# Loading x a body ahead and placing its vector steps elsewhere in a conditioned mixture-of-experts layer

## The reference

```python
q = relu(cond @ W3 + b3)                       # one row of 512 per sequence
h = relu(((64 * x + x.sum(axis=1)) * q) @ W2 + b2)
scores = softmax(h @ gate_w.T)                 # 64 experts
w, i = top_k(scores, 6)
# a token takes one of an expert's 64 places in order of its number; later ones are dropped
y = sum over its experts of w * ((silu(h @ w_gate[e]) * (h @ w_up[e])) @ w_down[e])   # inner width 352
shared = (silu(h @ sw_gate) * (h @ sw_up)) @ sw_down                                  # inner width 704
return x + y + shared
```

## Time and profile before

| | |
|---|---|
| median of 3 runs | 1281.77 us (1281.76 to 1282.28) |
| the profiled execution | 1281.53 us, its span 1279.7 us |
| PE busy | 1234.2 us, 96% |
| DVE busy | 708.8 us, 55% |
| ACT busy | 351.7 us, 27% |
| mean granted clock of TensorE | 0.995 |
| opening | 0 to 51.59 us |
| body 0, from its first gate and up tile | 51.59 to 112.02 us |
| bodies 1 to 6 | 112.02 to 576.21 us |

### The profile page before, as it was taken

The page is one execution under the profiler, slowest core; times in us unless marked ns, Lnnn a source line. Parts: engine busy times, 40 slices in busy tenths (PEclk is TensorE's granted clock), DMA queues, the critical chain, the costliest instruction groups (busy, mean ns, idle before and its releaser), DMA issues.

```text
span 1279.7 us, 15745 instructions
## 1 busy us (share of the span) xinstructions
PE 1234.2 (96%) x5944; PEld 913.4 (71%) x5944; DVE 708.8 (55%) x1368; ACT 351.7 (27%) x656; POOL 146.2 (11%) x118
## 2 busy tenths in 40 slices
PE   5999898998989999999999999999999999999998
PEld 5877677887878778788867666666666666666666
DVE  6888896978879788795823233232232323323322
ACT  3644243332434235244212111121111201211110
POOL 0000000000000000000002222221222222212221
PEclk9999999999999999999999999999999999999999
DMA  8925516264271544515758978979979888888853
GB/s 184 230 77 152 120 54 166 53 174 98 74 188 49 144 91 137 135 54 154 287 196 282 288 257 291 319 231 288 328 226 328 308 252 282 278 295 278 294 125 79
DMA packets 157179, 250.89 MB, mean 196 GB/s; under 512 B 21488, under 2 KB 92272, under 8 KB 155952
## 3 DMA queue, kind: packets, MB, share of 16 engines
q1 hardware_dynamic: 145040, 223.67, 55.3%
q0 software_dynamic: 11488, 25.17, 9.6%
q10 hardware_dynamic: 576, 1.05, 0.2%
HBM read 197.14 MB, written 61.10 MB: 202 GB/s over the span
## 4 chain that ended last, share of the span: by engine, by line
PE 63%; DVE 18%; issue 5%; DMA 5%; ACT 4%; SPq 4%; ACTq 0%; DVEq 0%
PE bank L1312 14%; PE bank L1314 13%; PE bank L1313 13%; PE bank L1508 12%; PE bank L1531 7%; DMA x<-in_x_dram 4%; DVE hrow L880 2%; DVE cand L972 2%; DVE x L860 2%; DVE x L851 2%; DVE first L967 2%; DVE prod L898 1%; DVE xpart L838 1%; SPq L381 1%; PE bank L1491 1%
## 5 line engine op out<-in xcount | busy, mean ns | idle before, releaser
L1312 PE MATMUL bank<-hh,gu 128*128 128x512 f32 x704 | 284.6, 404 | 22.4 <-DVE outst L915 18.0
L1313 PE MATMUL bank<-hl,gu 128*128 128x512 f32 x704 | 277.1, 394 | 0.0
L1314 PE MATMUL bank<-hh,gu 128*128 128x512 f32 x704 | 276.8, 393 | 0.0
L1312 PEld LDWEIGHTS bank<-hh,gu 128*128 128x128 f32 x704 | 134.0, 190 | 66.1 <-DVE outst L915 20.5
L1314 PEld LDWEIGHTS bank<-hh,gu 128*128 128x128 f32 x704 | 133.8, 190 | 29.3
L1313 PEld LDWEIGHTS bank<-hl,gu 128*128 128x128 f32 x704 | 133.9, 190 | 25.5
L898 DVE TENSOR_TENSOR prod<-bank,prod 128x512 f32<-128x512 f32 x96 | 65.8, 686 | 149.1 <-PE bank L1314 127.4
L612 ACT ACTIVATE ah<-prod 128x512 fp32r<-128x512 f32 x96 | 60.5, 631 | 290.4 <-DVE prod L898 290.4
L1312 PE MATMUL bank<-sdh,ah 128*128 128x512 f32 x320 | 126.8, 396 | 0.0
L1313 PE MATMUL bank<-sdl,ah 128*128 128x512 f32 x320 | 124.6, 390 | 0.0
L1314 PE MATMUL bank<-sdh,al 128*128 128x512 f32 x320 | 124.6, 389 | 0.0
(11 more groups left out here) (114 smaller groups left out, 1621.8 us busy)
## 6 DMA issues: line engine op xcount, KB each, us to landing
wg<-in_L_ffn_w_gate_dram SPq DMA_DIRECT2D x64, 704.0 KB
wu<-in_L_ffn_w_up_dram SPq DMA_DIRECT2D x64, 704.0 KB
wd<-in_L_ffn_w_down_dram SPq DMA_DIRECT2D x64, 512.0 KB
table<-hrow SPq DMA_DIRECT2D x64, 256.0 KB, 4.3
x<-in_x_dram SPq DMA_DIRECT2D x60, 256.0 KB, 7.0
wd<-in_L_ffn_w_down_dram SPq DMA_DIRECT2D x64, 192.0 KB
out_dram<-outst SPq DMA_DIRECT2D x36, 256.0 KB, 2.4
outst<-in_x_dram SPq DMA_DIRECT2D x32, 256.0 KB, 3.7
```

The source lines that it names most:

```text
L1312: nc.tensor.matmul(o, st_h, mv_h, start=first_mm, stop=False)
L1313: nc.tensor.matmul(o, st_h, mv_l, start=False, stop=False)
L1314: return nc.tensor.matmul(o, st_l, mv_h, start=False, stop=last_mm)
```

## The change

What it does, part by part:

- **Loads of x.** In body i, `load_x(d)` comes first on SP, where `load_x(c)` stood. Where `load_x(d)` stood, later, after `load_xr(i, 0)` and `(i, 1)`, there is now `load_x(d + 1)`, which is the next body's c.
- **x's steps.** In bodies 1 to 6, the five DVE steps of the first half of c stood after the low parts of h of b, between the `take_rows`; they now stand among these low parts. `score(a)` comes after the third low part instead of the second. `take_down(v-1, 3)` moves before the last two `take_rows`.
- **Routing in two parts.** `route` ends with `z`; the rest (ranks) is `mark`. For chunk b, `product(v, 0)` stands between them.
- **A silu table.** After `exp_scores(a)` in bodies 1 to 7, ACT runs silu on one element of `spare`.
- **Body 0.** The low part of the last weight piece, `split_piece(8)`, moves from before to after `product(v, 5)` and `split_a(v, 5)`.
- **Opening.** The eight small loads of b3 and b2 go from SP's queue to the front of ACT's. The loads of x(0) are split around the load of W2. After the products for `q`, PE does 32 transposes of the identity into a bank that nothing reads.

```diff
+            def load_x(n, half=None):
...
-            load_x(0)
+            load_x(0, 0)
...
             load_piece(0)
+            load_x(0, 1)
             load_x(1)
...
+                if d < NCH:
+                    load_x(d)
                 if i > 0:
-                    if c < NCH:
-                        load_x(c)
                     store_out(i - 1, 2)
                     load_xr(i - 1, 3)
...
+                    store_scores(a)
+                    store_rows(b)
+                    store_out(i - 1, 3)
+                    load_xr(i, 0)
+                    load_xr(i, 1)
...
+                if d + 1 < NCH:
+                    load_x(d + 1)
                 store_scores(b)
...
+            def silu_table():
+
+                nc.scalar.activation(spare[:, 1:2], spare[:, 0:1], ACT.Silu)
...
+                for b, c in ((b3, b3c), (b2, b2c)):
+                    for q in range(P // SQ):
+                        act.dma_start(c[q * SQ:(q + 1) * SQ, :],
...
                         exp_scores(a)
+                        silu_table()
...
+            def mark(n):
...
                 for oc in range(KC):
                     if i == 0 and oc == 1:
                         split_piece(2)
+                    if 0 < i < ND - 1 and oc < 3:
+                        (x_turn, x_sum, x_pair)[oc](c, 0)
                     split_h(b, oc)
-                    if i > 0 and oc == 1:
+                    if i > 0 and oc == 2:
+                        if more:
+                            x_shift(c, 0)
                         score(a)
...
+                elif more:
+                    x_scale(c, 0)
...
-                    x_turn(c, 0)
                     take_rows(b, 0)
-                    x_sum(c, 0)
                     take_rows(b, 1)
-                    x_pair(c, 0)
+                    take_down(v - 1, 3)
                     take_rows(b, 2)
-                    x_shift(c, 0)
                     take_rows(b, 3)
-                    x_scale(c, 0)
-                    take_down(v - 1, 3)
...
                     route(b)
                     product(v, 0)
+                    mark(b)
...
-                split_piece(8)
                 product(v, 5)
                 x_turn(d, 0)
                 split_a(v, 5)
+                split_piece(8)
...
+            for _ in range(32):
+                nc.tensor.transpose(bank[7][:, 0:P], ident[:, :], ident[:, :])
```

More of the change, by code:

```diff
@@ L141, in adaln_moe_ffn_kernel @@
         rsum = keep("rsum", [P, J])
+        spare = keep("spare", [P, 2])
         first = keep("first", [P, CAP])
@@ L373, in _ @@
         def _(sp):
-            def load_x(n):
+            def load_x(n, half=None):
                 if n >= 2:
                     sp.wait_ge(s.xml_ready, 2 * (n - 1))
[L377 to L382, removed]
+                b = slice(0, NB) if half is None else slice(half * (NB // 2), (half + 1) * (NB // 2))
+                rows = xf[n * CH + b.start * SQ:n * CH + b.stop * SQ, :].rearrange("(b i) d -> i b d", i=SQ)
+                for q in range(P // SQ):
+                    sp.dma_start(x32[q * SQ:(q + 1) * SQ, n % 2, b, :], rows[:, :, q * P:(q + 1) * P]).then_inc(
+                        x_loaded[n % 2] if half is None else x_begun[half], 16)
             def keep_x(n):
@@ L445, in load_down @@
                     sp.dma_start(wd[e][0:ITAIL, IT - 1, :], src[(IT - 1) * P:I, :]).then_inc(down_in[e], 16)
[L447 to L453, removed]
-            load_x(0)
+            sp.dma_start(conds[:, :], cond).then_inc(s.cond_loaded, 16)
+            sp.dma_start(w3s[:, :, :], W3.rearrange("(k p) o -> p k o", p=P)).then_inc(s.w3_loaded, 16)
+            load_x(0, 0)
             def load_piece(n):
@@ L476, in body @@
                 a, b, c, d = 2 * i, 2 * i + 1, 2 * i + 2, 2 * i + 3
+                if d < NCH:
+                    load_x(d)
                 if i > 0:
-                    if c < NCH:
-                        load_x(c)
                     store_out(i - 1, 2)
                     load_xr(i - 1, 3)
-                if i == 0:
-                    load_x(d)
+                    store_scores(a)
[3 more added lines that the diff above has]
+                    load_xr(i, 1)
+                else:
                     load_xr(i, 0)
@@ L677, in split_piece @@
                     copy(h_part, src).then_inc(s.piece_split_h, 1)
+            with nc.allow_non_contiguous_dma(reason="two vectors of 512 elements, once"):
+                for b, c in ((b3, b3c), (b2, b2c)):
+                    for q in range(P // SQ):
+                        act.dma_start(c[q * SQ:(q + 1) * SQ, :],
+                                      b[q * P:(q + 1) * P].rearrange("(k j) -> j k", j=SQ)).then_inc(s.bias_loaded, 16)
             act.wait_ge(s.condT_filled, 1)
@@ L691, in _ @@
             op.then_inc(s.q_ready, 1)
+            act.wait_ge(s.presets, 4)
             split_xm(0, 0)
@@ L988, in body @@
                     route(a)
+                    mark(a)
                 for oc in range(KC):
@@ L1218, in _ @@
             nc.vector.memset(zrows[:, 0:ROW], 0.0).then_inc(s.zero_rows, 1)
+            nc.vector.memset(spare[:, :], 0.0).then_inc(s.presets, 1)
             nc.vector.memset(cand[:, 0:CAP], 0.0).then_inc(s.presets, 1)
@@ L1221, in _ @@
             nc.vector.memset(zx[:, :, E:E + 2], SENTINEL).then_inc(s.presets, 1)
-            dve.wait_ge(s.presets, 3)
+            dve.wait_ge(s.presets, 4)
             dve.wait_ge(s.consts_ident, 2)
```

## The result

| | before | after |
|---|---|---|
| median | 1281.76 us (4 runs) | 1250.76 us (4 runs, 1249.95 to 1252.05) |
| the profiled execution, its span | 1281.53, 1279.7 us | 1252.05, 1250.3 us |
| PE busy | 1234.2 us, 96% | 1229.3 us, 98% |

The ratio is 0.976, with a 95% interval of 0.9748 to 0.9773: 31.0 us less. 1252.5 was predicted, in a range of 1246 to 1265.

A forecast was written before the change was run, and what follows sets the result against it. PE bounds the kernel, losing 31.5 us in bodies 1 to 6 around waits for take_down, late through x's load. Gains 1.1 + 1.6 + 4.4 + 4.7 + 17.6 = 29.4 us gave 1252.1 profiled, 1252.5 forecast, range 1246 to 1265.

The forecast's parts named there:

- the length derived from tiles of 2.73 us: Body 3: 77.41 us less 3.57 of waiting and 1.75 lost behind it, so 72.1 us of PE.
- Rival (2): Bodies 1 to 6: DVE's rate decides, bodies keep 2 us each, 12 less gain, 1264 us; chance 0.12.
- the third rival: Bodies 1 to 6: DVE enters late, low parts of h behind x's steps make PE wait, 1294 us; chance 0.03.
- The 0.5 us for a late low part of h: Body 1: 0.5 us of loss stays because DVE enters this body 2 us late.
- gets DVE some 2 us late from body 1: Body 2: DVE's lateness and two more rounds put product(v, 3) at T+46.2, 1.2 us late; gain 4.7 us.
- (c): Opening: W2 lands before x's second half, so W2's low parts start at 17.5 instead of 18.24; gain 0.7 us.
- the 0.4 for ACT's earlier steps behind the transposes: Opening: faster first products bring ACT's two steps of chunk 0 earlier, freeing 0.4 us of DVE's chain.
- the 1.1 that did not come: Opening: total gain of 0.7 + 0.4 = 1.1 us, between -0.7 and 3.
- the signs named for it: Opening: PE starts its first h tile near 18.3 us and waits for xml at 33.5.
- -0.7 in the opening: Opening: if small pieces were the limit, x would be no earlier and the opening loses 0.7 us instead of gaining 0.7.

The follow-up runs named there:

- run 2: Changed kernel with x's steps, score and take_down back in their old places, the loads of x still a body ahead: 1250.83 us.
- run 3: Changed kernel with the loads of x back where they were before, x's steps still among the low parts of h: 1307.05 us (one execution).
- Run 9: Changed kernel with a separate semaphore for b2, so that q waits for b3's loads only: 1251.81 us.
- run 10: Changed kernel with q waiting for b3 only and x(0)'s second half loaded ahead of W2 again: 1250.03 us.
- run 8: Changed kernel with the eight bias loads back on SP's queue behind W3: 1253.28 us.
- run 7: Changed kernel with 72 transposes in the opening instead of 32: 1251.45 us.

## Why the prediction was right, and where not

**Right, with the mechanism.** The gain sits where the sum had it, in bodies 1 to 6, and at the length derived from tiles of 2.73 us: 72.1 predicted, 72.15 measured. The waits for `take_down` are gone, DVE waits there for `outst` instead, inside its cover, and the clock is at 1.00. Runs 2 and 3 show that the load is the cause. Rival (2), DVE's rate, cost nothing in bodies 2 to 6: DVE is 86% busy in body 4 and PE never waits. That the x steps' new place costs nothing held as well, with the condition named in the third rival: run 3 shows the wait that comes if they are late.

**Body 1** had 75.7 predicted, 75.5 measured, with waits of 0.59 at t = 6 and 1.48 at t = 10 where only one at t = 10 was expected. The 0.5 us for a late low part of h was no wait. The `outst` load landed about when predicted: `take_down` ended 21.8 us into the body, against 21.5.

**Body 2: the failed step is "gets DVE some 2 us late from body 1".** Body 1 itself lasts 3.3 us longer than 72.15, and in that time DVE catches up. Its timeline has it waiting for the logits when body 2 starts its routing:

```profile
190.45 0.42 DVE L940 TENSOR_TENSOR lg<-bank,lg 128x256 f32<-128x256 f32 x1 [0.83 <-ACT lg L606]
```

`product(v, 3)` starts at 229.29 and takes 0.68, so it is ready 44.1 us into the body, not 46.2, and PE wants it at 45.0. A delay that PE has waited for is paid; I counted it twice. The term was 1.1 too small.

**Opening: the failed terms are (c), the split of x(0) around W2's load, put at 0.7, and the 0.4 for ACT's earlier steps behind the transposes.** Together they are the 1.1 that did not come; the signs named for it, PE's first tile of h at 18.3 and its wait for `xml` at 33.5, were 19.09 and 34.63. For (c), three landings were later than taken. `q` was to be ready at 12.6 and was at 14.0 (11.79 and 2.2 for its four steps), since its wait includes b2, whose loads landed 6.1 us after their issue. x's first half was to be used near 7 and was at 8.97. And its second half was used at 15.99, not near 15: a microsecond later, for which the prediction had put the term at 0. Run 9 shows that an earlier `q` alone doesn't matter, run 10 that with it x's second half does: W2 ahead of x costs 1.4 us there, and 1.7 between run 8 and the kernel before. Run 8 shows what the biases' move gives, some 2 us. In the changed kernel the two nearly cancel, 0.0 in the profiled executions, within the 0.8 by which openings differ.

The transposes were worth nothing. They were to end near 16 to 18 us, ended at 14.31, and PE's products from 19.09 on came as slowly as before the change. The 0.4 would not have come with a full clock either: run 7 had it in the first products, and the wait for `xml` ended no earlier.

The Trainium skill (DMA: Bandwidth & Descriptors, Issuing engines are not separate DMA queues) spoke for -0.7 in the opening, on the ground that another issuing engine saves only issue time. The trace agrees in part. SP issues x's first half 3.8 us earlier (at 1.66 instead of 5.50), but it is used only 0.9 us earlier, at 8.97 instead of 9.84. In the window of the earlier trace rows the DMA engines now have a share of 1.12 at 246 GB/s instead of 0.41 at 66:

```profile
4.50:7.50 3.00, 0.52 (x2) 0.55 (x3) 0.43 (x1) 2.19 (x3) 0.00 (x0) 1.00 1.12 246
```

A share under half in the kernel before was no sign that they would keep up once the loads come earlier. Still, the opening lost nothing, and with the biases back on SP it is 1.7 us longer (36.31 against 34.63).

**The median.** The profiled execution came out at 1252.05 where 1252.1 was predicted, by two errors of 1.1 us with opposite signs: the opening gave 1.1 less, body 2 1.1 more. That they cancel is luck. It is the longest of its four runs; the median lies 1.3 below it, where I had put it 0.2 above.

## What to carry to other kernels

When the longest wait is for a step at the end of an in-order chain, look for the transfer on which the first step of that chain stands, and issue it one round earlier if its buffer is free; with that done the order within the chain made no difference (run 2), and the new order without it cost 25 us (run 3). Sum the gain from body starts and the length of a body without waits, and don't carry a delay into the next body when the bottleneck has already waited for it. Then ask what is last in the queue of transfers: the next 1.5 us lay there, and moving one load ahead of another cost or gave more than any work on the clock.

## What the runs showed of the hardware that was not expected

- The same small loads land later on ACT's queue beside x than on SP's queue ahead of it. Which of the two, the queue or the company, does it, no run separates. Columns: out and source, queue, issues, KB each, us from issue to landing. In the changed kernel, on ACT's queue beside x:

```profile
b3c<-in_L_cond_b_dram ACTq DMA_DIRECT2D x4, 0.5 KB, 4.5
b2c<-in_L_cond_b_dram ACTq DMA_DIRECT2D x4, 0.5 KB, 6.1
```

  Before, on SP's queue ahead of x, the same loads took

```profile
b3c<-in_L_cond_b_dram SPq DMA_DIRECT2D x4, 0.5 KB, 2.7
b2c<-in_L_cond_b_dram SPq DMA_DIRECT2D x4, 0.5 KB, 2.4
```

- PE's clock was back at 0.50 after 4.8 us of standing, although 32 transposes had just run; with activity up to the first product it was 1.00 (run 7).
- The granted clock of a window can be wrong: in the kernel before, 23 products in 19 to 24 us come with a clock of 1.00, in the changed kernel as many with 0.50. The distance between starts, 0.21 us against 0.12, tells the level.
